# Width-8 attentions: row-tiled score pairs, and shifted scores that follow 28 slots after the plain ones

## The reference, cut to what matters

```python
# L1: plain.  L2: once for each of 4 experts, keys that are no members masked.  L3: rotary.
q, k, v = heads(x @ Wq + bq), heads(x @ Wk + bk), heads(x @ Wv + bv)   # 16 heads x 8
att = softmax(q @ k.T * scale (+ mask))                                # 256 x 256 for each head
x = x + gate * ((att @ v) @ Wo + bo)                                   # gate in L2 only
```

## Time and profile before

| what | us |
|---|---|
| median of three runs (2919.78 to 2929.6) | 2923.54 |
| the profiled execution, own time | 2921.03 |
| its span in the profile | 2919.3 |
| TensorE matmuls busy, share of the span | 87% |
| VectorE, ScalarE, GpSimd busy | 69%, 55%, 18% |

### The profile page before, as it was taken

The page is one execution under the profiler, slowest core; times in us unless marked ns, Lnnn a source line. Parts: engine busy times, 40 slices in busy tenths (PEclk is TensorE's granted clock), DMA queues, the critical chain, the costliest instruction groups (busy, mean ns, idle before and its releaser), DMA issues. The chain is left out here.

```text
span 2919.3 us, 72471 instructions
## 1 busy us (share of the span) xinstructions
PE 2552.9 (87%) x21324; PEld 1687.0 (58%) x21337; DVE 2011.4 (69%) x4949; ACT 1600.8 (55%) x3863; POOL 517.4 (18%) x1111
## 2 busy tenths in 40 slices
PE   5999999886999776658999999999999976999697
PEld 3777777553666444425666666666666643666354
DVE  6666666645887457747878788777887865888563
ACT  2555555422777423225777777777777762666531
POOL 2111111101221000001222222122222202333020
PEclk9999999986999886757999999999999996999799
DMA  4000000001222000002222222222222211222001
GB/s 129 1 0 0 0 0 0 1 1 42 74 72 72 7 1 0 0 6 75 77 72 72 74 73 74 72 72 75 73 72 72 74 32 50 72 70 69 7 1 29
DMA packets 123331, 128.40 MB, mean 44 GB/s; under 512 B 17401, under 2 KB 102221, under 8 KB 123214
## 3 DMA queue, kind: packets, MB, share of 16 engines
q1 hardware_dynamic: 123214, 126.94, 15.9%
HBM read 85.36 MB, written 39.88 MB: 43 GB/s over the span
## 5 line engine op out<-in xcount | busy, mean ns | idle before, releaser
L631 DVE TENSOR_REDUCE a_rowmax<-a_psS 128x2 f32<-128x512 f32 x1536 | 996.1, 685 | 291.7 <-PE a_psS L443 274.6
L561 ACT ACTIVATE a_probs<-a_psT 128x512 f32<-128x512 f32 x1536 | 882.4, 595 | 320.3 <-PE a_psT L455 292.5
L443 PE MATMUL a_psS<-stackk,stackq 65*128 65x256 bf16 x3072 | 608.3, 281 | 90.4 <-DMA stackk<-mask_dram 42.4
L455 PE MATMUL a_psT<-stackq,stackk 98*128 98x256 bf16 x3072 | 594.1, 275 | 16.9 <-ACT a_probs L561 5.1
L443 PEld LDWEIGHTS a_psS<-stackk,stackq 65*128 65x128 bf16 x3072 | 238.1, 99 | 320.4 <-DVE a_rowmax L631 183.9
L469 PE MATMUL a_psO<-a_probs,values 128*32 128x256 f32 x6144 | 413.7, 387 | 0.0
L455 PEld LDWEIGHTS a_psT<-stackq,stackk 98*128 98x128 bf16 x3072 | 276.5, 98 | 117.2 <-ACT a_probs L561 54.2
L893 ACT ACTIVATE a_probs<-a_psS,a_negmax 128x256 f32<-128x256 f32 x256 | 121.5, 475 | 256.7 <-DVE a_negmax L917 256.7
L469 PEld LDWEIGHTS a_psO<-a_probs,values 128*32 128x32 f32 x6144 | 160.8, 109 | 148.3 <-issue 72.7
L730 POOL TENSOR_SCALAR a_negmax<-a_rowmax 128x16 bf16<-128x16 f32 x192 | 48.7, 254 | 988.3 <-DVE a_rowmax L631 986.1
L569 ACT ACTIVATE a_oT<-a_psO 128x256 f32<-128x256 f32 x384 | 145.6, 379 | 44.4 <-PE a_psO L469 44.4
(11 more groups left out here) (206 smaller groups left out, 4199.3 us busy)
## 6 DMA issues: line engine op xcount, KB each, us to landing
a_scratch<-a_parts SPq DMA_DIRECT2D x96, 384.0 KB, 2.8
stackq<-a_scratch SPq DMA_DIRECT2D x192, 96.0 KB
stackk<-a_scratch SPq DMA_DIRECT2D x192, 96.0 KB
stackq<-a_scratch SPq DMA_DIRECT2D x192, 64.0 KB
stackk<-a_scratch SPq DMA_DIRECT2D x192, 64.0 KB
stackq<-a_scratch SPq DMA_DIRECT2D x192, 32.0 KB
stackk<-a_scratch SPq DMA_DIRECT2D x192, 32.0 KB
stackq<-a_negmaxT SPq DMA_DIRECT2D x384, 4.0 KB
```

The lines of the kernel that those rows point to most:

```text
L443: mm = pe.matmul(psS[h % 2][:, t * SEQ:(t + 1) * SEQ], stackq[0:MASK_ROW + 1, b, h, t * P:(t + 1) * P], stackk[0:MASK_ROW + 1, b, h, :], s ...
L455: mm = pe.matmul(psT[h % 2][:, t * SEQ:(t + 1) * SEQ], stackk[0:MAX_ROW + 2, b, h, t * P:(t + 1) * P], stackq[0:MAX_ROW + 2, b, h, :], sta ...
L561: act.activation(probs[:, h // 4 % 2, h % 4, :], psT[h % 2][:, :], ACT.Exp, scale=w.exp_scale).then_inc(exp_done, 1)
L631: dve.tensor_reduce(rowmax[:, s.parity(1), h, :], psS[h % 2][:, :].rearrange("p (t k) -> p t k", t=2), AX_X, ALU.max).then_inc(max_done, 1)
```

## The change

The computation is the same. What differs:

- **Row tiles.** A head's stack has 51 rows instead of 98: 48 of products, the mask's row (48), the maximum's two rows (49, 50). Two heads share the 128 partitions: one at rows 0 to 50, one at rows 64 to 114. `scores` and `shifted` are issued with `tile_position=(0, 0)` or `(64, 0)`. The heads are placed so that the plain scores of slot u and the shifted scores of slot u are always in opposite halves, and `score_pair` issues them interleaved (plain 0, shifted 0, plain 1, shifted 1).
- **28 slots apart.** In slot u, the shifted scores are those of head u + 4 of the job before (u < 12) or head u - 12 of the present one. `score_pair` waits for both the maxima and the exponentials of two slots back before it issues anything.
- **One piece per slot.** Every odd slot has half of a `prob_values` (8 passes, one value of t), every even slot one other piece: q, k, the maxima's transposes (once per job instead of twice), four transposes of the output (once instead of four times with two), v, y, and the output projection in two halves.
- **Fewer, wider steps on the other engines.** VectorE has two reciprocals, two products and two writes of values per job instead of four, four and one, and no more part in splitting q and k. ScalarE copies q and k out with the bias (two copies of 128 x 256; four in L3), and copies the output twice instead of four times. GpSimd does the whole split: copy, subtract, copy, subtract, and in L3 two products with the tables and a sum ahead of it.
- **Scratch.** It holds the stack's image, all six products: 6 writes per job, 4 loads (and one of the mask in L2). Stacks have four buffers, so the loads run a step ahead. `max_rows` has one wait and two transfers per job.
- **Depth.** The pipeline leads by 4 steps instead of 3 and drains over 2 instead of 1. `prob_values` is at offset -1, and `turn_output`, `turn_y`, `project_out` and `add_output` are at offset -2.

```diff
-    plan = Plan(jobs, weights, unroll, first, rounds=(jobs - 3 - first) // unroll, drain=1)
-    plan.misc_uses = [("o2", -1), ("m1", 0), ("o3", -1), ("v", 1), ("y", -1), ("o0", 0), ("m0", 1), ("out", -1), ("o1", 0)]
+    plan = Plan(jobs, weights, unroll, first, rounds=(jobs - LEAD - first) // unroll, drain=2)
+    plan.misc_uses = [("qk", 3)] + ([("qk2", 3)] if rotary else []) + [("m", 0), ("o", -2), ("v", 0), ("y", -2), ("out", -2)]
...
+        def place(h):
+            return h // 4 % 2, 4 * (h // 8) + h % 4
+        def shifted_head(u):
+            return (-1, u + 4) if u < 12 else (0, u - 12)
...
+            def save(s):
+                wait_alone(sp, parts_ready, s.n(3, 1, 1), sp_passed)
+                if s.known(3, 2):
+                    wait_alone(sp, stack_ready, s.n(2, stack_inc), sp_passed)
+                to = scratch[s.parity(3)].rearrange("qk product p t -> qk p product t")
+                for part, at, products in ((0, 0, 3), (1, 3, 2), (2, 5, 1)):
+                    sp.dma_start(to[0, :, at:at + products, :], parts[:, 0, 0:products, :]).then_inc(parts_saved, 16)
+                    sp.dma_start(to[1, :, at:at + products, :], parts[:, 1, part:part + 1, :].to_broadcast([P, products, SEQ])).then_inc(parts_saved, 16)
+            def stacks(s):
...
+                for g in range(2):
+                    rows = slice(GROUP_ROWS * g, GROUP_ROWS * g + MASK_ROW)
+                    sp.dma_start(stackq[rows, b, :, :], src[0, g, :, :, :]).then_inc(stack_ready, 16)
+                    sp.dma_start(stackk[rows, b, :, :], src[1, g, :, :, :]).then_inc(stack_ready, 16)
...
+            def step(s):
+                if s.has(2):
+                    stacks(s)
+                if s.has(0):
+                    max_rows(s)
+                if s.has(3):
+                    save(s)
...
+            def score_pair(s, u):
+                off, h = shifted_head(u)
+                if s.has(1):
+                    if u == 0:
+                        pe.wait_ge(stack_ready, s.n(1, stack_inc, stack_inc))
+                    if s.known(1, 1) or u >= 2:
+                        pe.wait_ge(max_done, s.n(1, HEADS, u - 1))
+                if s.has(off):
+                    if h == 0:
+                        pe.wait_ge(maxrow_ready, s.n(0, 32, 32))
+                    if s.known(off, 1) or h >= 2:
+                        pe.wait_ge(exp_done, s.n(off, HEADS, h - 1))
+                for t in range(2):
+                    if s.has(1):
+                        a = scores_part(s, u, t)
...
+                    if s.has(off):
+                        b = shifted_part(s, u, t)
...
+                for u in range(HEADS):
+                    score_pair(s, u)
+                    if u % 2 == 1 and s.has(-1):
+                        prob_values(s, u // 4, u // 2 % 2)
+                    if u == 0 and s.has(3):
+                        project_qk(s, "qk", 0, w.wq)
+                        if rotary:
+                            project_qk(s, "qk", 1, w.wk)
+                    if u == 2 and s.has(3):
+                        if rotary:
+                            project_qk(s, "qk2", 0, w.wq2)
+                            project_qk(s, "qk2", 1, w.wk2)
+                        else:
+                            project_qk(s, "qk", 1, w.wk)
+                    if u == 4 and s.has(0):
+                        turn_max(s)
+                    if u == 6 and s.has(-2):
+                        turn_output(s)
+                    if u == 8 and s.has(0):
+                        project_v(s)
+                    if u == 10 and s.has(-2):
+                        turn_y(s)
+                    if u in (12, 14) and s.has(-2):
+                        project_out(s, (u - 12) // 2)
...
+                for u in range(HEADS):          # ScalarE
+                    if u == 0 and s.has(-2):
+                        copy_oT(s, -2, 1)
+                    if u == 6 and s.has(0):
+                        copy_max(s)
+                    if u == 12 and s.has(-2):
+                        copy_yT(s)
+                    exponential(s, u)
+                    if rotary and u in (1, 2) and s.has(3):
+                        copy_qk(s, "qk", 0, u - 1)
+                    if u in (3, 4) and s.has(3):
+                        copy_qk(s, "qk2" if rotary else "qk", 1 if rotary else 0, u - 3)
+                    if u == 9 and s.has(-1):
+                        copy_oT(s, -1, 0)
...
+                for u in range(HEADS):          # VectorE
+                    if s.has(1):
+                        maxima(s, u)
+                    if u in (7, 8) and s.has(-2):
+                        normalise(s, u - 7)
+                    if u == 10 and s.has(0):
+                        write_values(s)
+                    if u == 15 and s.has(-2):
+                        add_output(s)
```

More of the change, by code:

```diff
@@ L262, in use @@
         step = self.at + off - uses[mine][1]
-        n = sum(0 <= at + o < self.plan.jobs for at in range(-3, step) for _, o in uses)
+        n = sum(0 <= at + o < self.plan.jobs for at in range(-LEAD, step) for _, o in uses)
         n += sum(0 <= step + o < self.plan.jobs for _, o in uses[:mine + 1])
@@ L276, in pipeline @@
 def pipeline(engine, plan, step):
-    for at in range(-3, plan.first):
+    for at in range(-LEAD, plan.first):
         step(Step(plan, at, None))
@@ L428, in project_v, with bank_of @@
+            def bank_of(s, kind, off):
+                bank, count = s.use(kind, off)
+                return shared[bank], misc_full[bank]
             def project_v(s):
[L429 removed]
+                ps, full = fill(s, "v", 0)
                 for t in range(2):
[L431 to L432 removed]
+                    mm = pe.matmul(ps[:, t * D:(t + 1) * D], xcur[:, s.quarter(0), t * P:(t + 1) * P],
+                                   w.wv[:, s.expert(0), :], start=True, stop=True)
@@ new lines, in prob_values @@
+            def prob_values(s, k, t):
+                half, i = k // 2, k % 2
+                if t == 0:
+                    if k == 0:
+                        wait_taken(pe, s, "v", -1)
+                    pe.wait_ge(exp_done, s.n(-1, HEADS, 4 * k + 4))
+                    if i == 0 and s.known(-1, 1):
+                        pe.wait_ge(oT_ready, s.n(-1, 2, half - 1))
+                for j in range(4):
+                    mm = pe.matmul(psO[half][SLOT * j:SLOT * (j + 1), 0:SEQ], values[:, s.parity(-1), t, 8 * i + 4 * half + j, :],
+                                   probs[:, 4 * k + j, t * SEQ:(t + 1) * SEQ], start=(t == 0 and i == 0), stop=(t == 1 and i == 1),
+                                   tile_position=(0, SLOT * j), skip_group_check=True)
+                if t == 1:
+                    mm.then_inc(pv_ready, 1)
@@ L494, in turn_y @@
                 mm.then_inc(full, 1)
-            def project_out(s):
-                wait_taken(pe, s, "y", -1)
-                ps, full = fill(s, "out", -1)
-                e = s.expert(-1)
-                for t in range(2):
-                    for k in range(3):
-                        pe.matmul(ps[:, t * D:(t + 1) * D], m.ones_bf[:, 0:P], w.bo_parts[:, k, e, :], start=(k == 0), stop=False)
-                    mm = pe.matmul(ps[:, t * D:(t + 1) * D], yT[:, t * P:(t + 1) * P], w.wo[:, e, :], start=False, stop=True)
-                mm.then_inc(full, 1)
@@ L506, in step, with project_out @@
-            def step(s):
-                for h in range(HEADS):
-                    if s.has(1):
-                        scores(s, h)
-                    if s.has(0):
-                        shifted(s, h)
-                    if h == 1 and s.has(-1):
-                        turn_output(s, -1, 2)
-                    if h == 2 and s.has(-1):
-                        prob_values(s, -1, 3)
-                    if h == 4 and s.has(0):
-                        turn_max(s, 0, 1)
-                    if h == 5 and s.has(-1):
-                        turn_output(s, -1, 3)
-                    if h in (6, 10, 14) and s.has(0):
-                        prob_values(s, 0, (h - 6) // 4)
-                    if h == 7 and s.has(1):
+            def project_out(s, t):
+                if t == 0:
+                    wait_taken(pe, s, "y", -2)
+                    ps, full = fill(s, "out", -2)
+                else:
+                    ps, full = bank_of(s, "out", -2)
+                e = s.expert(-2)
+                for k in range(3):
+                    pe.matmul(ps[:, t * D:(t + 1) * D], m.ones_bf[:, 0:P], w.bo_parts[:, k, e, :], start=(k == 0), stop=False)
+                mm = pe.matmul(ps[:, t * D:(t + 1) * D], yT[:, t * P:(t + 1) * P], w.wo[:, e, :], start=False, stop=True)
+                if t == 1:
+                    mm.then_inc(full, 1)
@@ L616, in rotary_half @@
-            def rotary_half(s, kind, which):
-                ps, taken = wait_full(dve, s, kind, 3)
-                if which == 0 and s.known(3, 1):
-                    dve.wait_ge(qk_summed, s.n(3))
```

(14 more changed lines are left out.)

456 lines of the change are left out of this document (205 added, 251 removed).

## The result

On the same chip the changed kernel took 2755.1 us (median of 4 runs, 2753.61 to 2758.91) and the kernel before 2924.99. The ratio is 0.9422, with a 95% interval of 0.9403 to 0.9441: 169.9 us less, where the sum of the prediction had 148. The profiled execution of the changed kernel took 2755.22 us, its span is 2753.5.

A forecast was written before the change was run, and what follows sets the result against it. TensorE was taken to bound the attentions before and after: 80 x 14.3 + 16 x 15.2 + 15 = 1402 us for 1590, so -188, +40 at the ends, -148 from 2921.03, stated as 2774 us; range 2690 to 2900.

The forecast's parts named there:

- The overlap: TensorE's scores: two heads in opposite halves stream together, so a slot's four passes take 0.22 us, not 0.44.
- third rival: TensorE's scores: tiles don't overlap in bf16, 3.5 us more a job, 3109 us in all; chance 0.06.
- The change of shape: TensorE: each change of tile shape costs 0.1 us, 32 times a job, where it was some 12 times.
- second rival: TensorE: changes of shape hide under waits, VectorE sets 13.0 us a job, 2648 us in all; chance 0.07.
- The waits kept: TensorE: 0.7 us a job of waits other than for stack loads remain, giving 14.3 a job, 15.2 in L3.
- first rival: `score_pair`: waits for maxima and exponentials couple, 2.0 us on top of 13.6 a job, 2898 us; chance 0.18.
- SyncE and the transfers: Transfers: no waiting within a step, about 41% busy; the maxima's rows cost 0 to 1 us a job, taken as 0.
- L3's job: L3's attention: two f32 matmuls more make TensorE's work 14.5 us, and a job 15.2 with waits.
- The ends: Stage ends: in front +2 us in L1 and L2, +9 in L3; behind +9 in each; together +40.
- The clock: Start of each stage's scores: the clock rises one third of a job later, 5 us more a stage.
- The mark of 0.95 or more: All three attentions: granted clock expected at 0.95 or more; below 0.9 the prediction would be wrong.
- fourth rival: TensorE's clock stays at half: 10 us a job more, 3700 us if in all jobs; chance 0.07.

The follow-up runs named there:

- experiment 1: Changed kernel with both kinds of scores of a slot taken from the same half, the half changing every four slots: 4076.16 us, 1.3843 of the kernel before.
- experiment 6: Changed kernel with all score passes untiled, over the rows of both heads of a pair: 2866.4 us, 0.9754 of the kernel before.
- experiment 5: Changed kernel with the wait for the exponentials moved between a slot's first plain and first shifted pass: 2760.99 us, 0.9394 of the kernel before.
- experiment 2: Changed kernel with TensorE's smaller pieces in L1 and L2 moved behind the odd slots' values, q and k joined: 2765.94 us, 0.9408 of the kernel before.
- experiment 7: Changed kernel with ScalarE instead of SyncE issuing the maxima's rows, in all stages: 2765.99 us, 0.9411 of the kernel before.
- experiment 9: Changed kernel with the smaller pieces in L1 and L2 moved behind the odd slots' values, one in each: 2781.04 us, 0.9472 of the kernel before.
- experiment 3: Changed kernel with SyncE issuing the maxima's rows ahead of the stacks' loads, in L3 alone: 2798.1 us, 0.9522 of the kernel before.
- the runs again: The changed kernel, unaltered, run again on the second and third chips: 2753.98 and 2755.01 us, 0.938 and 0.9388 of the kernel before.
- experiment 8: The kernel before with only the first 64 rows of a stack in both kinds of scores, untiled: 3016.62 us, 1.0272 of the kernel before.
- experiment 4: Changed kernel with a slot's scores issued plain, plain, shifted, shifted instead of in turns: 2757.83 us, 0.938 of the kernel before.

## Why the prediction was right, and where its sizes were off

- **The overlap** (0.22 for a slot's four passes, 0.32 to the piece): shown by the timeline after and, from the other side, by experiment 1 at full clock (0.55 to the piece from one half) and by experiment 6. The third rival is out.
- **The change of shape** at 0.1 a time, 32 times a job: measured at 0.1. q cost 0.63, and so did k (0.64 forecast), maxima 0.22 (0.2). The value piece was taken as 0.545 and is 0.58: eight times 0.035 is 0.3, so TensorE's work is 13.9, not 13.6. The Trainium skill, TensorEngine Tiling (Array Packing), Key Properties, says that a new mode drains the engine. The trace agrees, with 0.1 us each time. The second rival, under which the drains hide and a job takes 13.0, is out.
- **The waits kept** in L1 and L2, 0.7 a job: too many. A job of 14.15 less 13.9 leaves 0.25. Part of this was a slip: the terms for TensorE before the change add up to 15.35, not 15.2, so the waits before were 1.15 and what was left to keep 0.55. That the errors nearly cancel is luck: 14.3 stood in the sum. Sixteen and 64 jobs of it plus 5 each gave 234 and 920 us, measured are 228 and 907. The short first jobs of a stage (12.8 and 13.9, few pieces yet) were not in it.
- **Coupled waits** (first rival): the waits fell from 120.1 and 20.6 us in 57.4 jobs to 24.3 and 11.3 in 56.5, 0.6 a job where the rival had 2.0. That takes the rival out; experiment 5, which undoes only part of the coupling, would not. But the two engines are close to TensorE's pace: experiments 2, 7 and 9 each lengthened a job by 0.1 to 0.4 with a longer slot or some more work of ScalarE.
- **SyncE and the transfers.** No wait for stacks in L2, as forecast, at a DMA share of 0.35 and not 0.41. I put the maxima's rows at 0 of "0 to 1". In L1 and L2 that holds (3.7 us of waits in 56.5 jobs). In L3 it is the mis-sized term: 1.3 us a job, and 1.6 with the stop of 4.1 us. Its place is seen on SyncE's timeline in L3 after:

```profile
2404.65 0.82 SPq L404 DMA_DIRECT2D stackq<-a_scratch  x1
...
2407.03 0.68 SPq L405 DMA_DIRECT2D stackk<-a_scratch  x1
2408.63 1.41 SPq L382 DMA_DIRECT2D stackq<-a_negmaxT  x2
```

  The rows are issued last, at 2408.63, behind four loads of 192 KB (two shown). The trace has the loads' packets of 4096 bytes from 2406 to 2413.3 and the rows' packets of 512 bytes only from 2412.7 to 2413.2; the waiting scores start at 2413.86, on TensorE's timeline after:

```profile
2413.86 0.28 PE L461 MATMUL a_psS<-stackk,stackq 49*128 49x256 bf16 x1 [0.93 <-DMA stackq<-a_negmaxT]
```

  The stop of 4.1 us is the same delay: there the rows were issued at 2342.67, the loads' packets ran until 2347.8, the rows' began at 2346.9, and the scores of slot 12 started at 2348.59, 4.06 late. In L2 the loads are through at 1808.5 and the rows at 1809.1, and slot 12 comes at 1810.93: early enough by 1.8 us. L3 is later because its split is: GpSimd's chain of products, casts and subtractions ran from 2405.5 to 2415.1, some 10 us (11 forecast). I had given it "a step to hide under" and not asked what its writes, and so the loads, then collide with. Experiment 3 shows that the rows' wait is the loads ahead of them, and that they can't be put first from SyncE. The loads are needed at 2417.40, the next step's first scores, 4.1 us after their last packet; behind the rows they would be issued some 5.4 us later (2410.04 for 2404.65), an estimate from the rows above.
- **L3's job**, 15.2 forecast, is 16.05 and 16.4 to 16.5 in the runs again. The work is 14.8 (14.5 and the 0.3 of the value pieces; the shortest full jobs take 14.7 to 14.9), and the rows' 1.6 on top make 16.4, a little too much, since a part of it is idle time of weight loading. The stops also cost clock. In the profiled execution it fell once, behind the stop of 4.1 us, for 7 us (2346 to 2353). In the two runs again it fell four and three times in L3, for 21 and 17 us in all, each time behind a stop of 1.5 us or more for the rows. No term of the sum had this.
- **The ends**: +40 forecast, +38.9 measured, from first projection to first scores and from last scores to last update of x. In front L1 has +4.3 and L2 +4.7 (2 forecast each), L3 +1.8 (9 forecast): the six writes and the longer split together cost more in L1 and L2, and GpSimd's products in L3 cost little; which of them costs what was not taken apart. Behind, +8.7, +9.9 and +9.5 (9 each), but the working for it, 28 slots at 0.75 and 6 us, gives 27 and so +7. So the total is right and its parts are not, which is luck.
- **The clock**: +5 a stage forecast. The third job of L2 takes 18.8, 4.6 above a full one, and the upper level is reached 43 us into the scores, 24 before. This differs from run to run: in the two runs again it is reached 33 us into them and the third job takes 15.4, 1.2 above a full one. The mark of 0.95 or more in all three attentions is missed in L1 (0.91, and 0.93 in the runs again) and L3 (0.92, and 0.89 and 0.90), where the same delay lies in a stretch a quarter as long. In L3 of the runs again the clock is below the 0.9 that the prediction named as a sign of being wrong; it lost time there, but far from what the fourth rival priced. In the changed kernel the fourth rival did not come. That it is near, experiment 1 shows.

What holds the clock down in experiment 1 is not shown. Its score passes use one half at a time and change shape twice in a slot. Experiment 8 has one half with fewer changes, the changed kernel has the changes with both halves, and both are at the upper level but for the start of each stage and the short falls in L3. The two together were at the lower level for all of L1 and L2, and then at the upper one for the last 139 us of L3, so together they don't decide it either. No experiment varied one of them alone inside this kernel.

## What to carry to other kernels

Two heads in opposite halves of the array doubled the rate of these short contractions (four passes in 0.22 us for 0.44), but each slot of them pays a change of shape on the way in and out: count the slots, and expect a gain only where the neighbour has another shape than the whole array anyway, as the values here. Spread the other pieces evenly, one per slot; saving changes of shape by joining pieces cost more in waits than it saved (0.3 to 0.4 us a job). When a producer becomes longer but "hidden", follow what it triggers: here a small, urgent transfer that came to stand behind 768 KB of loads, which in turn had only 4 us to spare. And count what a stop does to the clock: in L3 it fell behind stops of 1.5 to 4.1 us.

## What the runs showed of the hardware that was not expected

- The granted clock stayed at 0.50 for 1930 us in which matmuls were busy for 1927 (experiment 1); the changed kernel, with another half for every second pass, has 0.98. In L3 of the same run it rose to 1.00 at 3791 us and stayed there to the end of the stage.
- The clock fell within L3 behind stops of TensorE of 1.5 to 4.1 us, for 3.4 or 6.8 us each time (the changed kernel's three profiles), and eleven times behind stops of 1.7 to 4.5 us (experiment 3). Not every such stop had a fall behind it: one of 1.8 us at 2396 in the first profile had none.
- Passes in different row tiles overlap also when the program has two of one tile first: 0.01 us apart (experiment 4).
- An ordinary matmul over 64 rows pays for a change of shape like a tiled one: 0.31 for two passes before an untiled piece, where passes over 98 rows take 0.22, and 0.75 us more a job (experiment 8).
